# Slot sums by rounds of four blocks, ten or eleven picked tiles by turns, and contiguous source rows in a graph-network kernel

## The reference

```python
h = jnp.maximum(_layernorm(x, axis=-1), 0.0)
def _nnconv(x, src, dst, edge_attr, ew, eb, rw, rb):
    W = (edge_attr @ ew + eb).reshape(edge_attr.shape[0], x.shape[1], rw.shape[1])
    xj = x[src]
    msg = jnp.einsum('ei,eio->eo', xj, W)
    agg = jax.ops.segment_sum(msg, dst, num_segments=x.shape[0])
    return agg + x @ rw + rb
# layers 0 and 1: h = relu(batchnorm(nnconv(h)))
# layer 2:        h = relu(nnconv(h));  out = x + h @ pred_w + pred_b
```

## Time and profile before

| | us |
|---|---|
| median of 3 runs | 7477.99 |
| lowest, highest | 7477.64, 7480.97 |
| the profiled execution, its own time | 7481.76 |
| its span, first to last instruction | 7478.8 |
| mean granted TensorE clock | 0.977 of full speed |
| busy: PE, DVE, POOL, ACT | 7244.2, 5851.7, 5326.7, 4981.2 |

### The profile page before, as it was taken

One profiled execution on the slowest core, in us unless ns is written; L12 is line 12 of the kernel. 1 busy time (PEld: TensorE's weight loads), 2 busy tenths in 40 slices (PEclk: granted clock), 3 DMA queues, 4 the chain that ended last, 5 costly groups with the idle time before them and its releaser, 6 DMA issues.

```text
span 7478.8 us, 138584 instructions
## 1 busy us (share of the span) xinstructions
PE 7244.2 (97%) x53192; PEld 6608.9 (88%) x53192; DVE 5851.7 (78%) x7566; ACT 4981.2 (67%) x8367; POOL 5326.7 (71%) x5635
## 2 busy tenths in 40 slices
PE   4999999999999999999999999999999999999998
PEld 1999999999999699999999999968999999999998
DVE  3888878787878678788888888867888888787885
ACT  3666666666666566666666666656666666666665
POOL 4677777777777377777777777737777777777772
PEclk7999999999999799999999999979999999999998
DMA  8111111111111111111111111111111111111110
GB/s 39 29 31 31 31 31 31 31 31 30 30 31 31 27 29 31 31 31 31 31 31 31 31 31 31 31 26 30 31 31 30 32 29 31 31 31 31 31 31 21
DMA packets 783276, 229.34 MB, mean 31 GB/s; under 512 B 643869, under 2 KB 733869, under 8 KB 782619
## 3 DMA queue, kind: packets, MB, share of 16 engines
q1 hardware_dynamic: 529252, 172.27, 11.0%
q0 software_dynamic: 180000, 46.44, 7.3%
q10 hardware_dynamic: 73367, 1.76, 1.0%
HBM read 216.52 MB, written 3.52 MB: 29 GB/s over the span
## 4 chain that ended last, share of the span: by engine, by line
PE 85%; DVE 7%; issue 4%; DVEq 3%; DMA 1%; ACT 0%; ACTq 0%
PE bank L1076 68%; PE bank L1043 10%; DVE xbig L639 3%; DVEq L720 3%; PE bank L1032 2%; PE bank L1091 1%; DVE agg L725 1%; DVE spread L684 1%; PE bank L1090 1%; PE bank L1101 1%; PE bank L1103 1%; DMA key_all<-in_src 1%; PE bank L1148 1%; PE bank L1160 1%; DVE xg L689 0%
## 5 line engine op out<-in xcount | busy, mean ns | idle before, releaser
L469 POOL DMA_INDIRECT xg<-node_table,idx x5625 | 5325.9, 947 | 2036.1 <-issue 1766.2
L1076 PE MATMUL bank<-nodes,low_hot 128*128 128x400 f32 x30000 | 5742.7, 348 | 68.9 <-DVE spread L684 52.2
L1076 PEld LDWEIGHTS bank<-nodes,low_hot 128*128 128x128 f32 x30000 | 5403.8, 188 | 279.0 <-issue 180.9
L915 ACT ACTIVATE distance<-key_all,low_id 128x640 bf16<-128x640 int16 x3000 | 2242.9, 818 | 1912.7 <-issue 1219.7
L684 DVE TENSOR_TENSOR spread<-mask,bank 128x400 f32<-128x400 uint8 x3750 | 1989.0, 564 | 1234.7 <-PE bank L1076 1234.5
L921 ACT ACTIVATE low_hot<-distance,one 128x640 fp32r<-128x640 bf16 x3000 | 2232.9, 817 | 0.0
L689 DVE TENSOR_REDUCE xg<-spread 128x80 f32<-128x2000 f32 x750 | 1677.0, 2236 | 25.7
L639 DVE TENSOR_TENSOR xbig<-xg,bank 128x1280 f32<-128x1280 f32 x750 | 1327.3, 1810 | 1.0 <-issue 0.2
L1043 PE MATMUL bank<-xbig,hot 128*32 128x144 f32 x18750 | 994.5, 295 | 0.0
L1043 PEld LDWEIGHTS bank<-xbig,hot 128*32 128x32 f32 x18750 | 820.6, 109 | 162.0 <-issue 99.1
L631 DVE TENSOR_TENSOR hot<-bank,dst_rel 128x800 f32<-128x800 f32 x375 | 367.8, 981 | 0.0
(11 more groups left out here) (109 smaller groups left out, 998.6 us busy)
## 6 DMA issues: line engine op xcount, KB each, us to landing
key_all<-edge_keys SPq DMA_DIRECT2D x375, 320.0 KB, 3.7
xg<-node_table,idx POOLq DMA_INDIRECT x5625
ea<-in_edge_attr SPq DMA_DIRECT2D x375, 100.0 KB
idx<-in_src SPq DMA_DIRECT2D x375, 7.5 KB
node_table<-rows_room SPq DMA_DIRECT2D x3, 781.2 KB
xbig<-node_table SPq DMA_DIRECT2D x9, 192.0 KB
xbig<-in_x SPq DMA_DIRECT2D x2, 781.2 KB
xbig<-in_dst ACTq DMA_DIRECT2D x1, 782.5 KB, 67.4
```

The lines of the kernel that those rows point to most:

```text
L469: pool.indirect_dma_start(out=xg[u][:, j, :], out_offset=None, in_=table[:, :], in_offset=bass.IndirectOffsetOnAxis(ap=idx[u][:, j:j + 1], ...
L915: nc.scalar.activation(distance[f][:, 0:tiles.stop - tiles.start, :], key[u % KEYS][:, tiles, :], ACT.Abs, bias=low_id[:, f:f + 1]).then_i ...
L1076: last = nc.tensor.matmul(p_sel[t % BANKS], low_hot[:, f, t, :], nodes[i][:, f, :, :].rearrange("p d f -> p (d f)"), start=(f, i) == (0, 1 ...
```

## The change

- **Sums by rounds.** `sum_tiles` is replaced by `sum_round`: in slot g PE sums only the rounds that end in it, whole, four blocks at a time; blocks of a round that has not ended wait for the next slot. The semaphore `s_seg` (slot summed) gives way to `s_round` (round summed), and who waited for a slot's sum now waits for all rounds up to that slot (`slot_summed`). `hot` gets a third buffer.
- **Ten or eleven picks.** `picks_of(g)` is 10 in even slots and 11 in odd ones; so many tiles are picked, and 15 or 14 gathered. The second part of the picks has 5 or 6 tiles. PSUM banks for picks go by the running number of the pick, not by its place in the slot. `low_hot`, `key`, `mask`, `fine`, `spread` and `distance` grow by the tile.
- **Contiguous source rows.** The last 1920 sources of each slot are loaded by one DMA, one row of 7680 bytes per slot on 125 partitions. The low bits become keys with copies only, and the upper bits (`fine`) are brought to edges-on-partitions by eleven transposes; `edge_keys` is written as one row of 2816 bytes per slot. `rows` moves into the third `xw` buffer.

The lists of DVE and ACT (`segments`, `copy_segments`) keep their order. The core of the diff:

```diff
+        def picks_of(g):
+            return MOST - 1 + g % 2
+        def parts_of(g):
+            return slice(0, RUN), slice(RUN, picks_of(g))
+        def picks_to(k):
+            return MOST + sum(picks_of(h % G) for h in range(k))
+        def slot_summed(eng, k):
+            if k >= 0:
+                eng.wait_ge(s_round, k // G * R + rounds_done(k % G))
...
-                        pool.wait_ge(s_seg, layer * G + b * SLOTS + (u + 1))
+                        slot_summed(pool, layer * G + b * SLOTS + u - SLOTS)
-                        for j in range(FETCHED):
+                        for j in range(TILES - picks_of(b * SLOTS + u)):
...
-                dve.wait_ge(s_seg, k + CREDIT - 1)
+                slot_summed(dve, k - 2)
-                onehots(hot[k % PAIR][:], dst_rel[:, n:n + BLOCKS, :].rearrange("p n j -> p (n j)")).then_inc(s_hot, 1)
+                onehots(hot[k % HOTS][:], dst_rel[:, n:n + BLOCKS, :].rearrange("p n j -> p (n j)")).then_inc(s_hot, 1)
...
-                dve.wait_ge(s_seg, k + CREDIT - 2)
-                products(xw[k % TRIPLE][:, TAKEN, :], xg[u][:, TAKEN, :], p_ea[k % PAIR][:, TAKEN, :])
+                slot_summed(dve, k - 2)
+                taken = slice(TILES - picks_of(b * SLOTS + u), TILES)
+                products(xw[k % TRIPLE][:, taken, :], xg[u][:, taken, :], p_ea[k % PAIR][:, taken, :])
...
-            for i in range(PICKED // RUN):
-                act.dma_start(src_pick[:, :, i * RUN:(i + 1) * RUN],
-                              src_b.rearrange("(g a) p j -> a p g j", a=BLOCKS)[FETCHED // RUN + i, :, :, :]
-                              ).then_inc(s_src, 16)
+            act.dma_start(src_c, src.rearrange("(g e) -> g e", g=G)[:, GE - LATER:GE]).then_inc(s_src, 16)
...
-                    act.wait_ge(s_seg, layer * G + g + (1 + CREDIT))
+                    act.wait_ge(s_round, n + 1)
...
-            def sum_tiles(g, buf, onehots):
+            def sum_round(layer, r):
+                n = layer * R + r
+                if n >= PAIR:
+                    pe.wait_ge(s_z, n - PAIR + 1)
+                blocks = range(r * GANG, min((r + 1) * GANG, NB))
                 for j in range(RUN):
-                    for a in range(BLOCKS):
-                        n, t = g * BLOCKS + a, a * RUN + j
-                        c = n % GANG
-                        done = nc.tensor.matmul(p_z[n // GANG % PAIR][c * WIN:(c + 1) * WIN, :], onehots[:, t, :],
-                                                buf[:, t, :], start=j == 0, stop=j == RUN - 1)
-                return done
+                    for i in blocks:
+                        k, t, c = layer * G + i // BLOCKS, i % BLOCKS * RUN + j, i % GANG
+                        last = nc.tensor.matmul(p_z[r % PAIR][c * WIN:(c + 1) * WIN, :], hot[k % HOTS][:, t, :],
+                                                xw[k % TRIPLE][:, t, :], start=j == 0, stop=j == RUN - 1)
+                last.then_inc(s_round, 1)
...
-                before = t - BANKS if t >= BANKS else max(range(t, PICKED, BANKS)) - PICKED
-                pe.wait_ge(s_taken, k * PICKED + (before + 1 + PICKED))
+                n = picks_to(k) + t
+                pe.wait_ge(s_taken, n - BANKS + 1)
...
-                        for t in range(PICKED):
-                            if not (last and u == SLOTS - 1):
+                        for t in range(MOST):
+                            if not (last and u == SLOTS - 1) and t < picks_of(g + 1):
                                 pick(layer, b, u + 1, t)
...
-                        behind = layer * R + ((g + 1) * BLOCKS - 1) // GANG - 1
-                        if behind > 0:
-                            pe.wait_ge(s_z, behind)
-                        sum_tiles(g, xw[k % TRIPLE], hot[k % PAIR]).then_inc(s_seg, 1)
+                        for r in rounds_of(g):
+                            sum_round(layer, r)
```

More of the change, by code:

```diff
@@ L18 @@
 BLOCKS = TILES // RUN
-PICKED = 10
-FETCHED = TILES - PICKED
+MOST = 11
+FETCHED = 15
 FOLD = 4
@@ L25 @@
 PAIR = 2
+HOTS = 3
 GANG = 4
@@ L111, in gnn_kernel @@
         one = sb("one", [P, 1])
-        fine = sb("fine", [P, G * PICKED], U8)
-        mask = [sb(f"mask{i}", [P, PICKED, FINE], U8) for i in range(PAIR)]
+        fine = sb("fine", [P, G * MOST], U8)
+        mask = [sb(f"mask{i}", [P, MOST, FINE], U8) for i in range(PAIR)]
         spread = sb("spread", [P, HALF, D, FINE])
@@ L269, in gnn_kernel @@
         s_prod = sem("products_ready")
-        s_seg = sem("segments_summed")
+        s_round = sem("round_summed")
         s_merge = sem("merge_onehot_ready")
@@ L326, in landed @@
         def landed(eng, layer, g):
-            eng.wait_ge(s_gath[g % SLOTS], (layer * BODIES + g // SLOTS + 1) * 16 * FETCHED)
+            eng.wait_ge(s_gath[g % SLOTS], 16 * sum(TILES - picks_of(h % G) for h in
+                                                    range(g % SLOTS, layer * G + g + 1, SLOTS)))
         def ends_quad(g):
@@ L494, in _ @@
                 dve.sem_inc(s_low, 1)
-            for _ in range(PICKED):
+            for _ in range(MOST):
                 dve.sem_inc(s_taken, 1)
@@ L678, in take_picks @@
                 k = layer * G + b * SLOTS + u
-                t0, t1 = PARTS[half].start, PARTS[half].stop
+                g = b * SLOTS + u
+                t0, t1 = parts_of(g)[half].start, parts_of(g)[half].stop
+                done, at = picks_to(k), TILES - picks_of(g)
                 dve.wait_ge(s_mask, k + 1)
@@ L929, in copy_picked_rows @@
                 act.wait_ge(s_xg, k * 2 + 2)
-                act.wait_ge(s_seg, k + CREDIT - 2)
-                nc.scalar.activation(xw[k % TRIPLE][:, TAKEN, 0:D], xg[u][:, TAKEN, :], ACT.Copy).then_inc(s_xc, 1)
+                slot_summed(act, k - 2)
+                taken = slice(TILES - picks_of(b * SLOTS + u), TILES)
+                nc.scalar.activation(xw[k % TRIPLE][:, taken, 0:D], xg[u][:, taken, :], ACT.Copy).then_inc(s_xc, 1)
             def copy_fetched_rows(layer, b, u):
@@ L982, in _ @@
                 pe.sem_inc(s_root, 1)
-                pe.sem_inc(s_seg, 1)
             pe.wait_ge(s_ident, 1)
-            pe.wait_ge(s_keyf, 1)
-            flat = key_f.rearrange("p g j -> p (g j)")
-            for c in range(PICKED):
+            pe.wait_ge(s_finef, 1)
+            for c in range(MOST):
                 if c >= 2:
-                    pe.wait_ge(s_key16, c - 1)
-                nc.tensor.transpose(bank[c % 2][0:G, 0:P], flat[:, c * G:(c + 1) * G], ident[:]).then_inc(s_keyT, 1)
+                    pe.wait_ge(s_fine, c - 1)
+                nc.tensor.transpose(bank[c % 2][:, 0:G], fine_f[:, c, :], ident[0:G, 0:G]).then_inc(s_fineT, 1)
             def find_bases():
-                pe.wait_ge(s_key16, PICKED)
+                pe.wait_ge(s_fine, MOST)
                 pe.wait_ge(s_base, 1)
@@ L1111, in segment_sums @@
                 apart(pe)
-                for t in range(PICKED):
+                for t in range(picks_of(0)):
                     pick(layer, 0, 0, t)
```

111 lines of the change are left out of this document (64 added, 47 removed).

## The result

The kernel takes 7572.76 us after the change (median of 4 runs, 7571.61 to 7573.88) and 7479.26 before it on the same chip (4 runs, 7477.64 to 7480.97). The ratio is 1.0124, interval 1.0108 to 1.0139: slower by 1.2%. The forecast was 7543 in a range of 7478 to 7610. The profiled span grew from 7478.8 to 7569.8, by 91.0 us.

What follows compares the result with a forecast made beforehand. PE was taken to bound the kernel, nearly balanced with POOL. Picks +92, sums -114 and DVE waits gave +28.3 us a layer, +85 in three; less 20 at the start, median 7543 us, range 7478 to 7610.

Steps and rivals of the forecast that it cites:

- Sums by rounds: Slot sums on PE: time follows the longest column group, 1.22 us saved in one-round slots, 114 us a layer.
- Rival 3: Slot sums on PE: time goes by records, a round takes 2.06 us, nothing saved, 7779 us; chance 0.02.
- rival 4: Slot sums on PE: passes with four groups busy cost a quarter more, 7627 us; chance 0.06.
- Ten and eleven tiles: Picks on PE: 62 odd slots pick one tile more at 1.48 us, 92 us more a layer.
- DVE doesn't follow: At `pick`: DVE's unchanged order delays tile 0's take, so PE waits; 30 x 1.22 + 0.2 + 13.3 us a layer.
- rival 1: At `pick`'s wait on `s_taken`: DVE takes tile 0 by 7.9 us, the waits vanish, 7393 us; chance 0.11.
- POOL does not set the pace: Edge phases: 14.5 gathers, 18.1 us a slot, only lengthen POOL's lead over PE.
- Rival 2: Edge phases: POOL set the pace, so 62 gathers less per layer count, 7225 us; chance 0.02.
- The term of k mod 4 = 3: At `pick`, k the slot just picked: DVE's 8.33 us list against PE's 7.90, wait 0.43 us, 31 times a layer.
- The term of k mod 4 = 1: At `pick`, `add_quad` in DVE's list, 10.19 us: all 1.22 us saved turns into wait, 30 times a layer.
- The term of the start: Start: fewer source packets let targets drain earlier, ACT is free near 69 instead of 89.5, 20 us gained.
- the cover gone: DVE's register loads no longer hide the six-tile reduce's extra 0.42 us before the adds: 38 us, bound 123.

Runs made afterwards that it cites:

- e1: Changed kernel with ten picked tiles in every slot, rounds and contiguous source rows kept: 7324.31 us, ratio 0.9789.
- e3: Changed kernel with ten and eleven picks by turns, but all 25 tiles of a slot summed in one run: 7743.44 us, ratio 1.0348.
- e4: Changed kernel with the quad's adds and their register loads moved between DVE's takes: 7382.17 us, ratio 0.9867.
- e5: Changed kernel with the eleventh tile in the first part of the picks (six, then five): 7546.01 us, ratio 1.0086.
- e6: Changed kernel with ten picks in every slot and the adds between DVE's takes: 7338.23 us, ratio 0.981.
- e10: Kernel before the change, with only the adds and their register loads moved between DVE's takes: 7371.7 us, ratio 0.9854.
- e8: Changed kernel with the contiguous source load issued by ACT only after x has landed: 7568.68 us, one run.
- e2: Changed kernel with ten picks and sums by slots again, leaving only source rows and new buffers: 7473.5 us, ratio 0.999.
- the fastest version: Changed kernel with adds between takes, loads beside first takes, five tiles first, eleven picks in chosen slots, sources after x: 7209.79 us, ratio 0.9636.

## Why the prediction was right

**Sums by rounds: right.** A round takes 1.36 us, two take 2.57 to 2.59 (forecast 1.35 and 2.57): a sum's time is that of its longest column group, the 32 columns of PE that one block uses. Rival 3 (sums by records, 2.06 a round) and rival 4 (four-wide passes a quarter dearer) fall; e1 shows the saving of 1.20 us in full at k mod 4 = 2. The Trainium skill's figure for three column tiles ("TensorE: Matmul & The Clock Gate", Part 3, measured speedup), by which rival 4 was weighed, does not show here: a pass takes 0.13 to 0.14 us either way (2.57 for 20 in the longest group, 1.36 for 10).

**Ten and eleven tiles: right.** 1.48 us a tile in e3 and in k mod 4 = 0 (21.51 for 20.05 in e1).

**DVE doesn't follow: right, and the step that decided.** From last pick to PE's restart it took 10.19 us at k mod 4 = 1 and 8.33 at k mod 4 = 3, both as forecast to the hundredth. One path was not in the working: at k mod 4 = 1 PE's transposes wait for DVE's adds (`transpose_round` waits on `s_add`), which takes 1.38 of the 1.90 us of idle time. It changed no time, as the take of tile 0 still ended last. e4 shows the cause: with the adds elsewhere, the same kernel is 191 us faster. That its 7382 is near rival 1's 7393 is chance. Rival 1 took out only the new waits (36.6 + 0.2 + 13.3 a layer), though by its own condition the old wait of 1.07 at k mod 4 = 1 had to go too, 30 x 1.07 x 3 = 96 us more; e4 took out the old wait and left the one at k mod 4 = 3. e5 shows that the six-tile reduce costs 0.42 us at k mod 4 = 3 and nothing at 1, behind the loads.

**POOL does not set the pace: right.** Rival 2's 7225 was wrong for the change as made; POOL waits 418 us. But e1, e6 and e10 show how near it is: with ten picks its lead is used up after 109 us saved (e10), and at 150 us (e1, e6) DVE waits for landings.

**Where the sum missed.** The change was forecast as +65 us and measured as +91 in the span (+93.5 in the medians): the direction and the mechanism held, the size was short by more than a quarter. The profiled execution was forecast as a span of 7544; it is 7569.8, 26 more. Slot 1's picks lie ahead of a layer's first slot sum, so of the forecast's terms 80.5 fall to the phases, -18.5 to the start and +3.0 to the gaps; against these the phases came out 24.8 higher (105.3), the start 6.3 higher (-12.2), gaps and tail 5.1 lower (-2.1). Per layer, by slots of one k mod 4, before to after (k mod 4 = 0, 1, 2, 3): +44.4, +2.0, +8.5, -19.8, where the forecast's terms give +44.4, -1.0, +8.1, -24.5.
- *The term of k mod 4 = 3 was mis-sized by 4.7 a layer.* The list was 8.33 long as forecast, yet the slot is 17.37 for 17.22. After a wait the 48 picks take 9.02 us in the chain, 188 ns each, where 185 had been taken from an unbroken run of 64. So such a wait costs 0.14 us beyond the list's length. The same shows where PE waits for nothing: the 16 picks behind each sum take 3.11 us, not 16 x 185 ns = 2.96. A run of picks that starts anew is some 0.15 us longer; the trace doesn't say why.
- *The term of k mod 4 = 1 by 3.0.* Of the 90 such slots behind a quad 72 are at 19.2 to 19.3, but 9 are at 19.6 and 9 at 20.3, which makes 4.4 us a layer. In both kinds DVE's queue stands 0.39 us at issue among the loads, or right behind them, and the adds start 0.36 us late; why it stands there is open. PE's wait for the adds is thereby 1.68 to 1.75 us for 1.38. At 19.6 that is all. At 20.3 the granted clock falls as well, by windows of one such slot, the 5 us after the wait and the rest:

```profile
1805.00:1810.00 5.00, 5.00 (x20) 4.85 (x19) 4.84 (x8) 0.38 (x2) 3.78 (x5) 0.66 0.33 52
1810.00:1818.55 8.55, 8.55 (x49) 8.29 (x47) 6.18 (x8) 5.87 (x8) 6.42 (x8) 1.00 0.08 6
```

A clock of 0.66 means that part of these 5 us ran at 1.2 GHz in place of 2.4. Over the slot PE is busy 18.6 us for 17.3, but DVE's take is then done before PE asks for it and the wait of 0.52 is gone, so the slot is 0.75 longer. All nine slots of this kind have 0.92 over the slot, all nine at 19.6 have 1.00, and so have the 72 others. So the longer wait was followed by a lower clock in half of its cases. The edge phases of the kernel before have no such stretch.
- *The term of the start was mis-sized:* 13.7 us (12.2 and the extra pick of slot 1) for 20. The working let all targets move "from about 20 us on". x lands at 17.2 for 12.9, beside the contiguous source load; the halves of the targets are issued at 21.0 and 24.9, and of the 80000 packets 5642 have moved by 25, where the working had 8250. From 25 on 1600 packets per us went, near the 1650 taken. That makes 71 to 72 us; the last 2400 packets of one half moved only between 72 and 77, for which the runs show no reason, and ACT was freed at 75.8, not at 69. e8 bears out that the source load holds x back: with it behind x the first slot sum starts 6.7 us earlier. The kernels with the same start and ten picks gained 14.2 (e1) and 15.7 us (e2), so up to 2 us of this term differ from kernel to kernel.

The forecast's own range, 7503 to 7601, held all this, though its bounds stood for other things (no 0.43 waits, the cover gone, a start that gains nothing), of which none came about in full. What it held was three smaller misses, two of them of terms that no bound had named.

## What to carry to other kernels

Before shortening a stretch of the busiest engine, measure for each kind of iteration how long the *other* engine's list is from the last thing it needs to the first thing it gives back. 1.2 us saved on PE was worth 1.2 us where that list was short, 0.66 where it was 8.33 us long (18.03 in e3, 17.37 after), and nothing where it was 10.19; moving 1.8 us of adds to a place where that engine waits anyway paid more (191 us) than the matmuls saved (171). Balance work between engines (here gathers against picks) last, slot by slot, and only where the engine that takes it has room: put into every second slot, while DVE held the slots between, the eleventh tiles cost 248 us (the kernel after against e1); some of them, in chosen slots of a kernel that POOL would otherwise hold, are part of the fastest version (fewer than one slot in three).

## What the runs showed of the hardware

- Four column groups of PE run at the price of one: 20 matmuls in four groups in 1.36 us, 25 with two blocks in one group in 2.57.
- Five register loads in DVE's queue take about 3 us (2.8 in the chain above). Behind a long reduce they run beside it and little is left (0.30 us); behind the one-hots of e4 they leave DVE standing for 2.30 us.
- A gather costs POOL 0.944 us and 0.305 us of issue, so once its lead is used up, 15 a slot set a floor of 18.75 us however fast the rest is: late in e1's layers four slots take 75.0 us.
- Waits of 1.38 us on PE left the granted clock at 1.00 in all 72 slots; of 18 waits of 1.68 to 1.75 us, 9 were followed by a stretch at 1.2 GHz that made the slot 0.75 us longer.
- 20-byte packets keep all 16 DMA engines busy: from 25 to 70 us 71805 packets, 1600 per us, and 1.88 MB in all.
